# A state-space mixer and a two-layer attention stack: more scan buffers, the output projection and the layer norm's averages as products of rounded parts, new step orders

## The chip, the core and the metric

The kernel runs as one program on one core of a Trainium2 chip. TensorE (PE) multiplies matrices into eight PSUM banks; VectorE (DVE), ScalarE (ACT) and GpSimd (POOL) do the elementwise work; SyncE (SP) starts the transfers. Each engine works through its own list of instructions in the order in which it was written, and waits where a semaphore has not yet been raised. The metric is the time of one execution on the device in microseconds (us).

## What is computed

Sixteen sequences of 512 tokens with 256 features go through a modulated layer norm, a selective scan (the mixer), a second norm, and two layers of a block with windowed attention and a gated hidden layer. Cut to what the change touches:

```python
# the mixer: 512 inner channels, 16 states per channel
h = exp(dt * A) * h + (dt * B_t) * x_t          # for each channel and state, along 512 tokens
y_t = sum over the states of h * C_t
x = x + ga * (((y + x_ssm * D) * silu(z)) @ W_out.T)

# each of two layers
q, k, v = split(shift_token(x) @ wqkv)          # 8 heads of 64
q, k = rotary(l2norm(q) * qs), rotary(l2norm(k) * ks)
o = local_attention(q, k, v)                    # windows of 128 tokens
x = x + o @ wo                                  # 512 -> 256
h = shift_token(x)
h = (h - h.mean(-1)) / sqrt(h.var(-1) + 1e-5) * lg + lb
a, g = split(h @ w1 + b1)
x = x + (a * gelu(g)) @ w2 + b2
```

## The kernel before

There are two phases, one after the other. Features lie on the partitions, tokens along the free dimension, unless said otherwise.

**The scan phase** (`mixer_pass`) takes 16 sequences in a pipeline. A pass has steps of three neighbouring sequences. The work of a sequence is cut into 32 units of 2 states and 128 channels, so a unit is 128x1024 elements. For each unit ACT makes the decays (L684), the input term is made on DVE (`mul`, L737, from a row spread by PE, L565) for 22 units and on POOL (L806, from rows in `b_wide`) for 10, DVE scans (L755), POOL multiplies by C (`cmul`, L813, from rows in `c_wide`), and PE sums the states in PSUM (`sum`, L573). When half the units of a sequence are summed, DVE multiplies the sums by the gate (`gate`, L761), twice two of them in a sequence; the output product `out` (L492) needs all four. `DECAY_SLOTS`, `STATE_SLOTS`, `C_SLOTS` and `B_SLOTS` say how many buffers each kind has. The order of all steps is one table of names, `MIXER_ORDER` (L139): each engine takes from it those steps that are its own, in the table's order; a `-` behind a name means the sequence before.

**The layer phase** (`stack_pass`) runs 32 passes, 16 for each layer. A pass has again steps of three sequences: q, k and v and their rotation for the next one, attention for the present one, and the output projection and the hidden layer for the last one. The table `ORDER` (L830) sets the order, and `BANK_OF` (L844) which PSUM bank each product uses. The steps that matter here, with their engine:

- `pq`, `pk`, `v` (PE, L1296): six products of 128x512. A float32 factor is split beforehand in an upper part, rounded to the format `float32r`, and a lower part, the rest; upper times upper, upper times lower and lower times upper are summed. `ga` (L1407) and `wd` (L1428) do the same for the hidden layer.
- `psq` (ACT, L1459) squares q and k into `qk_sq`, which is the same buffer as `qk_rot`; `pss` (DVE, L1669) sums; `pnorm` (DVE, L1680) writes `qk`; `prot` multiplies by the rotary tables on POOL (L1601) and on DVE (L1695); `padd` (DVE, L1701) adds; `ptr` (PE, L1326) turns.
- `score` (PE, L1346), `mask` (DVE, L1728), `exp` (ACT, L1506), `rate` (DVE), `pn` (POOL, L1628), `pt` (PE, L1357, copied by ACT and DVE), `att` (PE, L1373), `onorm` (DVE, L1759: one copy into `o_t` for each of four windows).
- `wo` (PE, L1286): the output projection, for each of two halves of the features four products in full float32. `add` (DVE, L1766, L1770): the residual, and after the second half the sum of both halves.
- `mean` (PE, L1387) and `var` (PE, L1392): one product each in full float32, with a matrix whose elements are all 1/256. Between them `cen` (DVE, L1785), `sq` (ACT, L1527), `sqs` (DVE, L1774); after `var` come `dev` (ACT), `xn` (DVE), `hn` (ACT), `hns` (DVE, L1650 and L1652) and `ga`.

## Time and profile before

| | |
|---|---|
| median of 3 runs | 4311.34 us (4310.83 to 4312.2) |
| the profiled execution | 4316.54 us, of which the span of its instructions is 4314.5 us |
| busy over the span | PE 4052.9 us (94%), DVE 3679.9 (85%), ACT 2672.4 (62%), POOL 2639.3 (61%) |
| mean granted TensorE clock | 0.981 |

A page says of each engine how long it was busy; the stretches by window show that the two phases have different limits, so shares over the whole span mislead. The scan phase ends at about 1780 us, the layer phase has the rest. A row of a timeline gives start, length, engine, line, operation, and how many instructions are merged; in brackets the idle time ahead of it and what ended it. Lengths of matmuls overlap (each is listed until its result is written), so what a group of them costs is the distance from its start to the start of what follows.

### The profile page before, as it was taken

The page shows a single profiled execution, that of the slowest core. Times are in us where ns is not written, and L with a number is a line of the kernel's source. Part 1 is how long each engine was busy: PE and PEld are TensorE (multiplying, and loading weights), DVE is VectorE, ACT ScalarE, POOL GpSimd, SP SyncE. Part 2 cuts the span into 40 slices and gives each one's busy share as a digit, 9 for nine tenths or more (in the row PEclk, how much of TensorE's full clock was granted, in tenths as well). Part 3 has the DMA queues.
Part 4 walks back from the last instruction along what each step waited for, and adds up shares of the span by engine and source line. Part 5 has one row for each costly group of instructions (what it writes and reads, how often), then busy time and mean ns, then how long its engine had stood idle before and what let it go on. Part 6 is the DMA issues. An engine that isn't in the chain of part 4 may idle for free.

```text
span 4314.5 us, 60081 instructions
## 1 busy us (share of the span) xinstructions
PE 4052.9 (94%) x19614; PEld 2629.3 (61%) x19614; DVE 3679.9 (85%) x5981; ACT 2672.4 (62%) x5767; POOL 2639.3 (61%) x1297
## 2 busy tenths in 40 slices
...
GB/s 96 108 118 121 123 120 118 118 118 119 122 118 118 121 121 112 144 78 35 16 27 19 26 21 25 21 17 63 29 68 21 35 26 27 33 25 35 20 30 25
DMA packets 118499, 295.02 MB, mean 68 GB/s; under 512 B 21208, under 2 KB 43664, under 8 KB 118192
## 3 DMA queue, kind: packets, MB, share of 16 engines
...
q8 instruction: 160, 2.62, 0.3%
...
## 4 chain that ended last, share of the span: by engine, by line
PE 34%; DVE 14%; issue 4%; ACT 4%; DMA 1%; SPq 0%; POOL 0%; DVEq 0%; ACTq 0%
PE b_bank L1407 12%; PE b_bank L1428 6%; PE b_bank L1296 5%; PE b_bank L1357 3%; PE b_bank L1373 3%; PE b_bank L1286 3%; ACT b_scores L1506 2%; DVE b_scores L1728 2%; DVE b_qk L1680 2%; DVE b_qk_rate L1669 2%; PE b_bank L1326 1%; PE b_bank L1346 1%; DVE b_qk_rot L1695 1%; DVE b_qk_rot L1701 1%; DVE b_xc L1785 1%
## 5 line engine op out<-in xcount | busy, mean ns | idle before, releaser
L813 POOL TENSOR_TENSOR a_state<-a_state,a_c_wide 128x1024 f32<-128x1024 f32 x512 | 1196.0, 2369 | 37.4 <-DVE a_state L755 37.4
L1628 POOL TENSOR_TENSOR b_scores<-b_scores,b_row_rate 128x1024 f32<-128x1024 f32 (+1 forms) x256 | 426.5, 1682 | 969.6 <-DVE b_row_rate L1745 969.6
L573 PE MATMUL a_y_sum<-a_state,a_ident 128*128 128x512 f32 x2048 | 942.3, 598 | 0.7 <-POOL a_state L813 0.6
L755 DVE TENSOR_TENSOR_SCAN a_state<-a_decay,a_slot 128x1024 f32<-128x1024 f32 x352 | 788.9, 2271 | 1.9 <-ACT a_decay L684 0.6
L1296 PE MATMUL b_bank<-b_w_qkv,b_hx_part 128*128 128x512 f32 x2304 | 661.7, 426 | 35.2 <-DVE b_w_qkv L1830 16.2
L1506 ACT ACTIVATE b_scores<-b_scores,b_row_bias 128x256 f32<-128x256 f32 (+1 forms) x1024 | 478.0, 469 | 269.9 <-DVE b_row_bias L1734 269.9
L573 PEld LDWEIGHTS a_y_sum<-a_state,a_ident 128*128 128x128 f32 x2048 | 387.1, 191 | 401.0 <-issue 342.4
L684 ACT ACTIVATE a_decay<-a_dt,a_neg_a 128x512 f32<-128x512 f32 x704 | 458.8, 711 | 164.0 <-DVE a_state L755 163.8
L1407 PE MATMUL b_bank<-b_hn_part,b_w 128*128 128x512 f32 x2112 | 515.4, 399 | 25.6 <-DVE b_hn_part L1652 25.6
L1296 PEld LDWEIGHTS b_bank<-b_w_qkv,b_hx_part 128*128 128x128 f32 x2304 | 424.0, 193 | 157.7 <-issue 48.2
L1601 POOL TENSOR_TENSOR b_by_cos<-b_qk,b_rotary 128x1024 f32<-128x1024 f32 x128 | 336.7, 2631 | 252.0 <-DVE b_qk L1680 249.9
L1407 PEld LDWEIGHTS b_bank<-b_hn_part,b_w 128*128 128x128 f32 x2112 | 397.4, 189 | 134.4 <-DVE b_hn_part L1652 40.8
L737 DVE TENSOR_TENSOR a_slot<-a_u,a_slot 128x1024 f32<-128x1024 f32 x352 | 417.2, 1213 | 24.6 <-PE a_slot L565 24.5
L806 POOL TENSOR_TENSOR a_state<-a_u,a_b_wide 128x1024 f32<-128x1024 f32 x160 | 375.9, 2369 | 27.6 <-PE a_y_sum L573 26.4
L684 ACT ACTIVATE a_slot<-a_dt,a_neg_a 128x512 f32<-128x512 f32 x320 | 208.0, 682 | 273.1 <-DVE a_state L755 272.4
L1635 POOL TENSOR_TENSOR b_h_part<-b_h,b_h_part 128x512 fp32r<-128x512 f32 x160 | 205.2, 1291 | 267.9 <-ACT b_h_part L1571 267.9
L755 DVE TENSOR_TENSOR_SCAN a_state<-a_slot,a_state 128x1024 f32<-128x1024 f32 x160 | 357.9, 2269 | 6.7 <-ACT a_slot L684 6.4
L1728 DVE CUSTOM_DVE_ANT_0 b_scores<-b_bank,b_squares 128x256 f32<-128x256 f32 (+1 forms) x1024 | 337.5, 385 | 3.4 <-issue 3.4
L1428 PE MATMUL b_bank<-b_h_part,b_w 128*128 128x512 f32 x1088 | 296.2, 406 | 0.0
L1802 DVE SCALAR_TENSOR_TENSOR b_h<-b_bank,b_b_1a,b_gelu 128x512 f32<-128x512 f32 x192 | 143.4, 747 | 167.5 <-POOL b_h_part L1635 64.3
L565 PE MATMUL a_slot<-a_bc_parts,a_picks 96*128 96x512 bf16 x704 | 213.4, 386 | 69.0 <-DVE a_state L755 67.6
L1357 PE MATMUL b_bank<-b_squares,b_scores 128*128 128x128 f32 x1792 | 265.2, 277 | 12.3 <-DVE b_qk L1680 7.9
...
## 6 DMA issues: line engine op xcount, KB each, us to landing
a_c_wide<-bc_rows SPq DMA_DIRECT2D x256, 512.0 KB, 3.7
...
```

The source lines that it names most:

```text
L573: last = nc.tensor.matmul(y_sum[dd][:], ident[:], state[state_ring.slot[q]][:, i, :], start=False, stop=(j == GROUPS - 1 and i == GROUP - 1))
L684: last = nc.scalar.activation(to[:, i, :], dt[slot][:, d, :], ACT.Exp, scale=neg_a[:, d, n:n + 1])
L737: nc.vector.tensor_tensor(slots[q % 2][:], u[slot][:, d, :].unsqueeze(1).to_broadcast([P, GROUP, SEQ]), slots[q % 2][:], ALU.mult).then_in ...
L755: nc.vector.tensor_tensor_scan(flat(h), flat(factor), flat(term), 0.0, ALU.mult, ALU.add).then_inc(scan_done.sem, 1)
L813: nc.gpsimd.tensor_tensor(h[:], h[:], c_wide[c_ring.slot[q // 2]][:], ALU.mult).then_inc(cmul_done.sem, 1)
L1296: last = nc.tensor.matmul(psum.tile(name)[:], x[:, c, w * P:(w + 1) * P].bitcast(F32R), weights[:, c, cols:cols + INNER].bitcast(F32R), st ...
L1357: last = nc.tensor.transpose(psum.tile(name)[:, n * P:(n + 1) * P], scores[w % 2][:, h, blk * WINDOW:(blk + 1) * WINDOW], ident)
L1407: last = nc.tensor.matmul(psum.tile(f"{stem}{m}")[:], weights[:, c, at * P:(at + 1) * P].bitcast(F32R), x[:, c, :].bitcast(F32R), start=(n ...
L1428: last = nc.tensor.matmul(psum.tile(f"wd{m}")[:], weights[:, k, m * P:(m + 1) * P].bitcast(F32R), x[:, held, :].bitcast(F32R), start=(k == ...
L1506: e = nc.scalar.activation(scores[w % 2][:, h, lo:hi], scores[w % 2][:, h, lo:hi], ACT.Exp, bias=row_bias[:, w, h:h + 1], accum_out=row_su ...
L1628: nc.gpsimd.tensor_tensor(probs, probs, row_rate[:, w, at].unsqueeze(2).to_broadcast([P, 4, hi - lo]), ALU.mult)\
L1728: last = nc.vector.tensor_tensor_reduce(out=scores[w % 2][:, head, lo:hi], in0=psum.tile(f"s{w}_{g}_{h}")[:, at + lo:at + hi], in1=mask[:, ...
```

## The change

In the scan phase there are 4 decay buffers for 3, and 3 of each kind of row buffer for 2, and `MIXER_ORDER` is another table. In the layer phase `wo`, `mean` and `var` become sums of products in `float32r`: `wo` has 12 products a half for 4, `mean` and `var` 2 for 1 (the matrix has no lower part, since 1/256 is exact). So `onorm` becomes two instructions, a rounding copy by ACT and a subtraction by DVE; `add` and `sqs` get a rounding copy and a subtraction each on DVE; `w_o` is split once per layer. `qk_sq` is now the same buffer as `qk` rather than `qk_rot`. To make room, buffers share memory: the input rows `hx` with the upper part of the normalised rows, `x_res` with the lower part, and loads of `hx` and `x_res` wait for the last `ga` product that reads those. `ORDER` and `BANK_OF` are new.

```diff
-DECAY_SLOTS, STATE_SLOTS, C_SLOTS, B_SLOTS = 3, 6, 2, 2
+DECAY_SLOTS, STATE_SLOTS, C_SLOTS, B_SLOTS = 4, 6, 3, 3
...
-sum-:5 bcast-:10 sum-:6 mul-:12 mul-:13 xload:0 bcast-:11 scan-:12 cload-:13 cload-:14 cload-:15 scan-:13 cload:0
+scan-:10 scan-:11 cmul-:6 cmul-:7 scan-:12 scan-:13 bcast-:13 bcmid-:0 xT-:1 xs-:0 xscopy-:3 xs-:1 decay-:19 soft-:0
...
-qk_sq = qk_rot
+qk_sq = qk
...
+sum_parts, sq_parts = ([x[:, c, :] for c in range(CHUNKS)] for x in (hn_upper, hn_lower))
...
 def load_hx(s, slot, layer, _):
-    sp.wait_ge(v_done.sem, v_done.at(s))
+    if s < 3 or s == BATCH:
+        sp.wait_ge(v_done.sem, v_done.at(s))
+    if s >= 3:
+        sp.wait_ge(g_full.sem, g_full.at(s - 3, HID_CHUNKS))
...
 def load_res(s, slot, layer, _):
-    sp.wait_ge(x2_done.sem, x2_done.at(s))
     if s == BATCH:
+        sp.wait_ge(x2_done.sem, x2_done.at(s))
         load_w_o(1)
+    if s > 0:
+        sp.wait_ge(g_full.sem, g_full.at(s - 1, HID_CHUNKS))
...
 def project_out(s, slot, layer, m):
-    product(s, f"wo{m}", w_o, m * P, [o_t[:, p, :] for p in range(PAIRS)])
+    parts = [(weights, x, p) for weights, x in ((w_o[0], upper), (w_o[1], upper), (w_o[0], lower)) for p in range(PAIRS)]
+    for n, (weights, x, p) in enumerate(parts):
+        last = nc.tensor.matmul(psum.tile(f"wo{m}")[:].rearrange("p (a f) -> p a f", a=2),
+                                weights[:, p, m * P:(m + 1) * P].bitcast(F32R), x[p].bitcast(F32R),
+                                start=(n == 0), stop=(n == len(parts) - 1))
...
+def averaged(s, name, parts):
+    for n, x in enumerate(parts):
+        last = nc.tensor.matmul(psum.tile(name)[:], mean_mat[:].bitcast(F32R), x.bitcast(F32R), start=(n == 0), stop=(n == 1))
...
 def square_qk(s, slot, layer, w):
-            act.wait_ge(qk_sum_done.sem, qk_sum_done.at(s, w))
+            act.wait_ge(by_cos_done.sem, by_cos_done.at(s, w))
+            act.wait_ge(by_sin_done.sem, by_sin_done.at(s, 2 * w))
...
+def copy_out(s, slot, layer, w):                      # on ACT
+    nc.scalar.activation(o_upper[:, :, w * WINDOW:(w + 1) * WINDOW].bitcast(F32R),
+                         psum.tile(f"o{w}")[:].rearrange("p (n c) -> p n c", c=WINDOW), ACT.Copy).then_inc(o_upper_done.sem, 1)
...
 def copy_out(s, slot, layer, w):                      # on DVE
-    nc.vector.tensor_copy(o_t[:, :, w * WINDOW:(w + 1) * WINDOW], psum.tile(f"o{w}")[:].rearrange("p (n c) -> p n c", c=WINDOW))\
-        .then_inc(o_t_done.sem, 1)
+    dve.wait_ge(o_upper_done.sem, o_upper_done.at(s, w + 1))
+    nc.vector.tensor_tensor(o_lower[:, w // 2, :, at:at + WINDOW].bitcast(F32R),
+                            psum.tile(f"o{w}")[:].rearrange("p (n c) -> p n c", c=WINDOW),
+                            o_upper[:, :, w * WINDOW:(w + 1) * WINDOW], ALU.subtract).then_inc(o_t_done.sem, 1)
...
 def cut_hx_of(s):
+    if s > 0:
+        dve.wait_ge(v_full.sem, v_full.at(s - 1, TILES))
...
 def times_sin(s, slot, layer, w):
+    dve.wait_ge(k_t_full.sem, k_t_full.at(s, w))
...
+def cut_sum(s, x, parts, signal):                     # called by add_residual and add_squares
+    upper, lower = parts
+    dve.wait_ge(signal.sem, signal.at(s, 1))
+    nc.vector.tensor_copy(upper.bitcast(F32R), x).then_inc(signal.sem, 1)
+    dve.wait_ge(signal.sem, signal.at(s, 2))
+    nc.vector.tensor_tensor(lower.bitcast(F32R), x, upper, ALU.subtract).then_inc(signal.sem, 1)
```

**First place, DVE in the scan phase, where one sequence's last units end.** `a_slot<-a_u,a_slot` is `mul`, `a_state<-...` a scan, `a_u<-a_y_sum,a_sz` a `gate`. Before:

```order
L737 TENSOR_TENSOR a_slot<-a_u,a_slot 128x1024 x2
L755 SCALAR_TENSOR_TENSOR a_state<-a_decay,a_slot 128x1024 x2
L737 TENSOR_TENSOR a_slot<-a_u,a_slot 128x1024 x2
L761 TENSOR_TENSOR a_u<-a_y_sum,a_sz 128x512
L755 SCALAR_TENSOR_TENSOR a_state<-a_decay,a_slot 128x1024
L761 TENSOR_TENSOR a_u<-a_y_sum,a_sz 128x512
```

and now:

```order
L738 TENSOR_TENSOR a_slot<-a_u,a_slot 128x1024 x2
L756 SCALAR_TENSOR_TENSOR a_state<-a_decay,a_slot 128x1024 x2
L738 TENSOR_TENSOR a_slot<-a_u,a_slot 128x1024
L756 SCALAR_TENSOR_TENSOR a_state<-a_decay,a_slot 128x1024
L738 TENSOR_TENSOR a_slot<-a_u,a_slot 128x1024
L762 TENSOR_TENSOR a_u<-a_y_sum,a_sz 128x512 x2
```

The next sequence's first scan has moved from between the two gates to ahead of both. In PE's list the last three sums stood behind both of the next sequence's first spreads; now they stand between and behind them.

**Second place, DVE in the layer phase, from `cen` to `sqs`.** Before:

```order
L1785 TENSOR_TENSOR b_xc<-b_x,b_bank 128x512 x2
L1708 COPY b_k_t<-b_bank 128x4x128
L1725 MEMSET b_waiter 128x1
L1728 ISA b_scores,b_row_max<-b_bank,b_squares 128x256
L1728 ISA b_row_max 128x1
...
L1774 TENSOR_TENSOR b_h<-b_h 128x512
L1669 TENSOR_REDUCE b_qk_rate<-b_qk_rot 128x16
```

and now:

```order
L1865 TENSOR_TENSOR b_xc<-b_x,b_bank 128x512 x2
L1788 MEMSET b_waiter 128x1
L1791 ISA b_scores,b_row_max<-b_bank,b_squares 128x256
L1791 ISA b_row_max 128x1
...
L1804 COPY b_probs_t<-b_bank 128x512 x2
L1756 TENSOR_TENSOR b_qk_rot<-b_qk,b_rotary 128x16x32 x2
L1853 TENSOR_TENSOR b_h<-b_h 128x512
L1847 CAST b_hn_part_16562<-b_h 128x512
L1849 TENSOR_TENSOR b_hn_part_16562<-b_h,b_hn_part_16562 128x512
```

Between `cen` and the squares' sum there stood one copy and one mask step; now a mask step, two copies and the rotation's sine products, and the cut of the sum follows it.

**Third place, PE in the layer phase, from `mean` to `var`.** Before:

```order
L1387 MATMUL b_bank<-b_rstd,b_squares 128x512
L1296 MATMUL b_bank<-b_w_qkv,b_hx_part 128x512 x6
L1326 MATMUL b_bank<-b_squares,b_qk_rot 128x128 x8
L1296 MATMUL b_bank<-b_w_qkv,b_hx_part 128x512 x6
L1357 MATMUL b_bank<-b_squares,b_scores 128x128 x4
L1296 MATMUL b_bank<-b_w_qkv,b_hx_part 128x512 x6
L1357 MATMUL b_bank<-b_squares,b_scores 128x128 x4
L1392 MATMUL b_bank<-b_h,b_squares 128x512
```

and now:

```order
L1429 MATMUL b_bank<-b_hn_part_16561,b_mean_mat 128x512 x2
L1381 MATMUL b_bank<-b_k_t,b_q_t 128x256 x4
L1392 MATMUL b_bank<-b_squares,b_scores 128x128 x16
L1329 MATMUL b_bank<-b_w_qkv,b_hx_part 128x512 x18
L1429 MATMUL b_bank<-b_hn_part_16562,b_mean_mat 128x512 x2
L1408 MATMUL b_bank<-b_probs_t,b_v 64x128 x8
```

All 16 turns of a window's probabilities now stand ahead of `var`, with 18 products of q, k and v, and the turn of q and k has moved behind it.

## Rows read from the trace of the kernel before

**Rows 1.** By window of 200 us: busy us of each engine, clock, DMA:
```profile
1000.00:1200.00 200.00, 188.13 (x566) 92.34 (x566) 194.73 (x126) 141.69 (x244) 193.08 (x88) 1.00 0.37 119
2400.00:2600.00 200.00, 197.52 (x1191) 148.74 (x1190) 166.60 (x411) 126.84 (x331) 81.00 (x46) 1.00 0.06 19
```

**Rows 2.** Waits from 300 to 1500 us: engine, for whom, us in total, times:
```profile
DVE a_u L761 <- PE a_y_sum L573: 20.0, 11, 1.9
DVE a_slot L737 <- PE a_slot L565: 6.6, 13, 1.4
POOL a_state L806 <- PE a_y_sum L573: 21.0, 19, 1.5
POOL a_state L813 <- DVE a_state L755: 18.5, 34, 0.8
```

**Rows 3.** Timeline of DVE, scan phase, a gate in two neighbouring passes; then POOL:
```profile
605.56 0.69 DVE L761 TENSOR_TENSOR a_u<-a_y_sum,a_sz 128x512 f32<-128x512 f32 x1 [1.89 <-PE a_y_sum L573]
711.81 0.69 DVE L761 TENSOR_TENSOR a_u<-a_y_sum,a_sz 128x512 f32<-128x512 f32 x1 [1.88 <-PE a_y_sum L573]
705.58 4.68 POOL L813 TENSOR_TENSOR a_state<-a_state,a_c_wide 128x1024 f32<-128x1024 f32 x2 [0.74 <-DVE a_state L755]
```

**Rows 4.** Waits of PE and DVE from 2000 to 4200 us:
```profile
PE b_bank L1407 <- DVE b_hn_part L1652: 16.2, 29, 0.6
DVE b_qk_rate L1669 <- ACT b_qk_rot L1459: 107.9, 59, 2.4
```

**Rows 5.** Timeline of PE, layer phase, one pass:
```profile
2210.91 11.45 PE L1407 MATMUL b_bank<-b_hn_part,b_w 128*128 128x512 f32 x48 [0.57 <-DVE b_hn_part L1652]
2249.81 3.70 PE L1286 MATMUL b_bank<-b_o_t,b_w_o 128*128 128x512 f32 x8
2252.94 3.36 PE L1296 MATMUL b_bank<-b_w_qkv,b_hx_part 128*128 128x512 f32 x12
2256.24 2.00 PE L1346 MATMUL b_bank<-b_k_t,b_q_t 64*128 64x256 f32 x16
2264.26 1.10 PE L1387 MATMUL b_bank<-b_rstd,b_squares 128*128 128x512 f32 x2
2266.64 1.44 PE L1326 MATMUL b_bank<-b_squares,b_qk_rot 128*128 128x128 f32 x8
2269.75 1.64 PE L1296 MATMUL b_bank<-b_w_qkv,b_hx_part 128*128 128x512 f32 x6
2271.22 0.60 PE L1357 MATMUL b_bank<-b_squares,b_scores 128*128 128x128 f32 x4
2271.66 1.02 PE L1392 MATMUL b_bank<-b_h,b_squares 128*128 128x512 f32 x2
2272.61 1.13 PE L1346 MATMUL b_bank<-b_k_t,b_q_t 64*128 64x256 f32 x8
2285.23 4.94 PE L1407 MATMUL b_bank<-b_hn_part,b_w 128*128 128x512 f32 x20 [0.55 <-DVE b_hn_part L1652]
```

**Rows 6.** Timeline of DVE in the same pass:
```profile
2250.52 0.69 DVE L1650 CAST b_hx_part<-b_hx 128x1024 fp32r<-128x1024 f32 x1
2264.03 1.29 DVE L1695 TENSOR_TENSOR b_qk_rot<-b_qk,b_rotary 128x512 f32<-128x512 f32 x2
2267.03 0.64 DVE L1741 COPY b_probs_t<-b_bank 128x512 f32<-128x512 f32 x1
2267.59 1.27 DVE L1785 TENSOR_TENSOR b_xc<-b_x,b_bank 128x512 f32<-128x512 f32 x2
2269.39 0.42 DVE L1728 CUSTOM_DVE_ANT_0 b_scores<-b_bank,b_squares 128x256 f32<-128x256 f32 x1
2270.78 0.71 DVE L1774 TENSOR_TENSOR b_h<-b_h 128x512 f32<-128x512 f32 x1
```

**Rows 7.** Timelines of DVE and of POOL, a sine product beside a cosine product:
```profile
2293.75 3.96 DVE L1695 TENSOR_TENSOR b_qk_rot<-b_qk,b_rotary 128x512 f32<-128x512 f32 x2
2294.30 2.85 POOL L1601 TENSOR_TENSOR b_by_cos<-b_qk,b_rotary 128x1024 f32<-128x1024 f32 x1
```

More of the change, by code:

```diff
@@ new lines @@
+mul-:27 cmul-:27 scan-:26 scan-:27 decay:8 sum-:24 bcast-:29 mul-:28 sum-:25 mul-:29 sum-:26 bcast-:30 mod:1 up:1
+sum-:27 scan-:28 bcast-:31 cload:7 scan-:29 dt-:1 mul-:30 sum-:28 cload:8 bcast:0 dtadd-:0 sum-:29 bcast:1 mul-:31
+sum-:30 decay:9 cmul-:28 scan-:30 cload:9 scan-:31 cmul-:29 sum-:31 bload:12 decay:10 decay:11 cmul-:30 dev2:0 mul:0
+skip:0 scan:0 mul:1 xcopy:1 out:0 bcast:2 gate-:2 gate-:3 xscopy:0 scan:1 decay:12 bcast:3 cload:10 scan:2 h2store:0
+cmul-:31 scan:3 sum:0 mul:2 res:0 bcast:4 bcast:5 out:1 mul:3 decay:13 cmul:0 sum:1 mul:4 cmul:1 h2:0 mean2:0 mul:5
@@ L160 @@
+bcast:6 xscopy:1 decay:14 dtadd-:1 cmul:2 cmul:3 scan:4 decay:15 xT:0 cstore:0 bcast:7 bcast:8 res:1 scan:5 cen2:0
+cload:11 sum:2 cmul:4 hT:0 mul:6 sum:3 cload:12 hT:1 mul:7 scan:6 hcut:0 cmul:5 sum:4 scan:7 xscopy:2 bccopy:0
+bload+:1 sum:5 bload+:4 decay:16 bcast:9 var2:0 bcast:10 cload:13 scan:8 sum:6 mul:8 scan:9 mul:9 mul:10 xn2:0 mul:11
+hcut:1 decay:17 bcast:11 cload:14 sum:7 bcup:0 decay:18 bcast:12
 """
@@ L829 @@
 ORDER = """
-ptr-:3 mask:0.0 mask:0.1 att-:3 score:0.0 exp:0 pn:0.0 hxs:0 hxload:0 psq:0 score:0.1 score:1.0 wo:0 mask:1.0 add:0
-prate:0 rate:0 pss:0 pnorm:0 pq:0 pk:0 pn:0.1 resload:0 score:1.1 mask:1.1 add:1 prot:0 score:2.0 exp:1 padd:0 wo:1
-pn:1.0 rate:1 v:0 pt:0.0 pt:0.1 cen:0 vc:0 ptc:0 sq:0 psq:1 mean:0 pk:1 ptr:0 pn:1.1 mask:2.0 sqs:0 pq:1 pt:1.0 v:1
-prate:1 pss:1 pt:1.1 vc:1 dev:0 pnorm:1 var:0 mask:2.1 score:2.1 pt:1.2 v:2 pt:1.3 pk:2 prot:1 xn:0 att:0 onorm:0
-att:1 padd:1 mask:3.0 score:3.0 vc:2 hn:0 exp:2 hns:0 gelu:0 score:3.1 onorm:1 psq:2 mask:3.1 ptr:1 gated:0 rate:2
@@ L835 @@
[L835 to L839 removed]
+ptr-:3 v-:3 hxs:0 mask:1.0 vc-:3 mask:1.1 score:0.0 score:0.1 score:1.0 hxload:0 exp:0 rate:0 add:0 pss:0 score:1.1
@@ new lines @@
+wo:0 psq:0 pk:0 x1load:0 pq:0 add:1 exp:1 rate:1 wo:1 v:0 pnorm:0 prate:0 v:1 pt:0.0 pn:0.0 pn:0.1 pt:0.1 vc:0 mean:0
+score:2.0 pt:1.0 cen:0 pn:1.0 mask:2.0 resload:0 pt:1.1 pn:1.1 store:0 sq:0 pt:1.2 pt:1.3 prot:0 psq:1 vc:1 pq:1 sqs:0
+pss:1 padd:0 xn:0 mask:2.1 pk:1 dev:0 v:2 prate:1 vc:2 var:0 ptc:0 hns:0 hn:0 pnorm:1 att:0 mask:3.0 score:2.1 onorm:0
+onorm:1 prot:1 rate:2 padd:1 gated:0 ptr:0 pn:2.0 gated:1 hl:0 pss:2 outstore:0 exp:2 mask:3.1 gelu:0 gelu:1 psq:2
+pn:2.1 pq:2 hl:1 gated:2 pnorm:2 att:1 score:3.0 hh:0 hh:1 gelu:2 pn:3.0 prate:2 hl:2 ptc:1 exp:3 prot:2 rate:3 ga:0
```

193 lines of the change are left out of this document (114 added, 79 removed).

## The prediction

> **What bounds the kernel now.** I read the windows first, because the two phases differ. In the scan phase three engines are nearly full at once: of 200 us DVE is busy for 194.7, POOL for 193.1 and PE for 188.1. In the layer phase only PE is: 197.5, beside 166.6 for DVE, 126.8 for ACT and 81.0 for POOL [rows 1]. So a microsecond of PE is worth nothing by itself in the first phase and nearly a microsecond in the second, where TensorE is also at its full clock, 1.00 [rows 1].
>
> The waits say what is left in the scan phase. A pass takes 711.81 - 605.56 = 106.25 us [rows 3]. In 1200 us, 11.3 passes, DVE waits 20.0 us for PE ahead of a gate and 6.6 us ahead of a `mul`, that is 1.8 and 0.6 us a pass; POOL waits 39.5 us, 3.5 a pass [rows 2]. DVE is the nearest to its bound: without waits its pass is 106.25 - 2.4 = 103.8 us, POOL's 102.8.
>
> A pass of the layer phase is 2285.23 - 2210.91 = 74.32 us from the first `ga` to the next one's first [rows 5]. PE waits about 0.57 us of it, at one place: ahead of `ga`, for DVE's cut of the normalised rows (16.2 us in 29 passes) [rows 4, 5]. So its work is 73.75 us. DVE waits a good deal, for instance 107.9 us for squares [rows 4], and no one is late through it.
>
> **What the PE work becomes.** The price of a `float32r` product is read from 48 of them in 11.45 us, 0.239 us each [rows 5]. The first half of `wo` and 12 such products take 2256.24 - 2249.81 = 6.43 us; less 12 x 0.239 = 2.87, four float32 products cost 3.56 us [rows 5]. Twelve `float32r` products will cost 2.87. That saves 0.69 us a half, 1.4 a pass. `mean` and six products take 2.38 us, so `mean` alone costs 2.38 - 1.43 = 0.95, and `var` 2272.61 - 2271.66 = 0.95 [rows 5]. Two products will cost 0.48: 0.47 us saved twice, 0.9 a pass. The sum is 2.3 us. Where products of this kind stand in small groups they cost a little more: six in 2271.22 - 2269.75 = 1.47 us, 0.245 each [rows 5]; by that price the saving is 2.1. I take 2.2 us a pass (ends 2.0 and 2.4), so PE's work becomes 71.55 us. Should PE wait as little as now, 32 passes give 70 us.
>
> **What DVE and ACT get.** The cut of a sum is a rounding copy of 512 elements and a subtraction. The copy of 1024 elements took 0.69 us [rows 6]; half of it lies between 0.35 and 0.69, I take 0.42, since the time of start is a small part there. The subtraction is like the sum of squares, 0.71 [rows 6]. Two cuts a pass are 2.2 us. `onorm` on DVE stays one instruction of 512 elements from PSUM. DVE's share rises from 83% of 74.3 us, 61.9 us, to 64.1 of some 73 us, 88%: no bound yet, but less slack. ACT gets four copies; a copy of that shape on DVE takes 0.64 [rows 6] and I take the same, 2.6 us a pass, which its 37% idle time takes [rows 1]. The split of `w_o` is a copy and a subtraction once per layer, 2 us each, at most 4 us in all; I take 1.
>
> **Where PE could wait now.** The saving is paid out only if the products find their factors ready. Between `mean` and `var` DVE has a chain. After `mean` (0.48 us) come `cen` 1.27, a mask step 2270.78 - 2269.39 = 1.39, two copies of 0.56 (2267.59 - 2267.03), sine products 1.29, the sum of squares 0.71 and its cut 0.42 + 0.71: 7.4 us [rows 6]. The squares on ACT are hidden beside the mask and the copies. PE has in the same stretch `mean` 0.48, eight score products 1.1, sixteen turns at 0.44 for four, 1.8, and eighteen products at 0.24, 4.4: 7.8 us [rows 5]. So the two are nearly even, where DVE had in the old order only `cen`, a copy and a mask step between, and PE 2271.66 - 2264.26 = 7.40 us [rows 5]. There is no slack to speak of, and every wait of DVE in this stretch will be PE's. Behind it, from `var` to `ga`, the same steps are as before, with less PE work between (the old stretch was 12.6 us [rows 5]). For `var`, `ga` and the turns of the probabilities, which now come sooner behind their exponentials, I take 1.3 us of waiting a pass in place of 0.57. The lower end is 0.6, as now; the upper is 3.2, if one of DVE's steps is blocked once a pass by POOL as in rows 7 (below).
>
> The layer pass then is 71.55 + 1.3 = 72.85 us, 1.47 less than now, and 32 passes give 47 us. The ends are 74.32 - (71.35 + 0.6) = 2.4 us a pass, 76 in all, and 74.32 - (71.75 + 3.2) = -0.6, a loss of 20.
>
> The other new waits are covered. The squares of q and k now wait for both rotary products of the window before, a chain of some 7 us a window, while four windows share 73 us. The cut of the input rows waits for the last `v` product, which PE has done before the scores, and DVE has two mask steps on those scores ahead of it. Loads of `hx` and `x_res` wait for the last `ga`, some 30 us ahead of their use.
>
> **What the scan phase becomes.** The engines' work is the same; only waits can go. At the gate, DVE in the old order had two `mul` steps after the last scan and then waited 1.88 us for PE, whose sums stood behind two spreads [rows 3]. In the new order a scan of another sequence stands ahead of both gates, and PE's sums come one spread sooner. The wait of 1.88 us goes. What is late next is the output product, since both gates are done some 1 us later; it has three scans of cover. The `mul` waits (0.6 us a pass) and POOL's waits for DVE [rows 2] I leave as they are, though more buffers for decays and rows let ACT and SP run further ahead; neither was the last to arrive in any row here. I take 1.5 us a pass, 24 us over 16 passes. The ends are 2.4 us, all of DVE's waits, 38 in all, and a loss of 10 us if the new order opens as large a wait at another place.
>
> **The sum.** 4316.5 us of the profiled execution, less 47, less 24, plus 1, is 4246.5. The median of the runs shown lies 5.2 us below that execution, so I forecast 4241 us.
>
> **Rivals.**
> *Layer phase without gain.* The chain from `mean` to `var` and the turns take back what the products save, in waits of 2.8 us a pass in place of 0.57. For it: the even balance above. Against it: rows 4 show that a chain of the same kind, just as tight, costs PE 0.57 us. The time is 4311 - 24 = 4287 us.
> *Both gains whole.* 4311 - 76 - 38 = 4197 us. Against it: the waits would have to shrink in both phases.
> *The scan order loses.* Some 5 us lost there and 47 won: 4269 us.
> *Slower, by blocking between DVE and POOL.* Two sine products that take 1.29 us took 3.96 where POOL's cosine product ran [rows 6, 7]: 2.67 us lost. The new cuts are DVE steps of that kind, both operands in SBUF, and the sine products now stand just ahead of the squares' sum, at the time of POOL's cosine product of the same window. If one such block a pass falls on the chain, the pass is 71.55 + 0.57 + 2.67 = 74.8 us, 15 us more over 32 passes, and with the scan's 24 the time is 4302, no change. If there are two, one at each chain, it is 77.5 us, 100 us more: 4387. It decides from 2.8 us of waiting a pass for the phase, and 3.5 for the whole. Against it: the sine products of rows 6 took their 1.29 us, so a block is not the rule, and POOL is busy for only 81 of 200 us here [rows 1].
> The Trainium skill, page "SBUF — State Buffer", section "SBUF: two separate sides", says that the port pair which VectorE and GpSimd share is an exclusive lock, taken by a VectorE step in a two-port mode or with two SBUF inputs for its whole length. Rows 7 agree with it. By that rule the rounding copies, and not only the subtractions, can be blocked; the sum stays, and the rule speaks for this last rival.
> *The saving is not there:* the products in `float32r` cost more with the new operands than rows 5 show. Then only the scan's gain is left, less the waits: near 4300.
>
> **How the numbers follow.** The forecast case has 0.60, 4241 us with 4205 to 4280; the layer phase without gain 0.12; both gains whole 0.06; the scan order losing 0.06; one block a pass, or no saving, 0.07; two blocks or another loss of that size 0.09. A measurement of this kernel can tell about 0.2%, 8.6 us. So faster has 0.60 + 0.12 + 0.06 + 0.06 = 0.84, the same 0.07, slower 0.09. The range of 4200 to 4293 holds the forecast case, the first and third rival, and some of the second: 0.8.
>
> **What would show it.** The scan pass should be near 104.7 us with no wait of 1.88 at the gates; the layer pass near 72.9. `wo` should cost 2.9 us a half, `mean` and `var` 0.5. PE's waits ahead of `var`, `ga` and the turns should sum to 1.3 us a pass; over 2.8 is the first rival, and sine products or cuts that last over 2 us are the fourth. The forecast is wrong if the scan pass is not under 105.5 us or the layer pass not under 73.8.

## The result, and the profile after

| | before | changed kernel |
|---|---|---|
| median | 4311.77 us (4310.83 to 4315.74, 4 runs) | 4197.57 us (4192.46 to 4202.05, 4 runs) |
| ratio, 95% interval | 1 | 0.9733 [0.9716, 0.975] |
| span of the profiled execution | 4314.5 us | 4192.1 us |

The kernel is 2.7% faster, 114 us by the medians. The forecast was 4241 us, and the range of 4200 to 4293 misses the time by 2.4 us. The rival "both gains whole" stood at 4197 with a chance of 0.06: its number is what came out, though not from the terms that it was added up from, as the part on the miss shows.

The two profiled executions are 122.4 us apart. The layer phase opens with a memset of VectorE, which starts at 1798.56 us before and at 1752.98 us now:

```profile
1752.98 0.06 DVE L1897 MEMSET b_hx<- 128x1 f32 x1 [4.72 <-PEq L225]
```

So 45.6 us come from the scan phase and its start, and 76.8 us from the layer phase. About 5 of the 45.6 lie ahead of the first gate, which DVE reaches at 130.52 us before and at 125.30 now; the last section shows that as much can lie between two executions with the same instructions up to there. The same windows as in [rows 1], busy us of PE, PEld, DVE, ACT, POOL:

```profile
1000.00:1200.00 200.00, 192.87 (x573) 93.48 (x572) 199.35 (x128) 139.91 (x244) 198.64 (x90) 1.00 0.37 122
2400.00:2600.00 200.00, 199.13 (x1251) 157.93 (x1248) 165.16 (x445) 136.80 (x348) 88.17 (x49) 1.00 0.06 19
```

In the scan phase DVE is idle for 0.65 us in 200 where it had 5.3. In the layer phase PE is idle for 0.9 where it had 2.5. The clock is 1.00 in both, so it is no part of the difference.

**Scan phase.** DVE's timeline, the two gates that answer to [rows 3], in neighbouring passes:

```profile
588.66 1.28 DVE L762 TENSOR_TENSOR a_u<-a_y_sum,a_sz 128x512 f32<-128x512 f32 x2
692.33 1.27 DVE L762 TENSOR_TENSOR a_u<-a_y_sum,a_sz 128x512 f32<-128x512 f32 x2
```

Both gates run back to back, with no idle time in brackets: the wait of 1.88 us is gone. The pass is 692.33 - 588.66 = 103.67 us for 106.25. The waits from 300 to 1500 us, that answer to [rows 2] (all that is left of DVE's, and two of POOL's):

```profile
DVE a_slot L738 <- PE a_slot L566: 2.8, 12, 0.2
POOL a_state L814 <- DVE a_state L756: 6.1, 11, 0.6
POOL a_state L807 <- PE a_y_sum L574: 2.8, 12, 0.3
```

**Layer phase.** PE's timeline of one pass, and the start of the next, that answers to [rows 5] (`wo` is L1422, `mean` and `var` L1429, `ga` L1457):

```profile
2329.70 2.13 PE L1422 MATMUL b_bank<-b_o_upper,b_w_o 128*128 128x512 f32 x8
2331.66 1.09 PE L1422 MATMUL b_bank<-b_o_lower,b_w_o 128*128 128x512 f32 x4
2332.59 2.96 PE L1329 MATMUL b_bank<-b_w_qkv,b_hx_part 128*128 128x512 f32 x12
2335.39 2.03 PE L1422 MATMUL b_bank<-b_o_upper,b_w_o 128*128 128x512 f32 x8
...
2342.27 0.72 PE L1429 MATMUL b_bank<-b_hn_part,b_mean_mat 128*128 128x512 f32 x2 [0.25 <-ACT b_probs_t L1569]
...
2350.39 0.70 PE L1429 MATMUL b_bank<-b_hn_part,b_mean_mat 128*128 128x512 f32 x2
2351.02 1.09 PE L1408 MATMUL b_bank<-b_probs_t,b_v 128*64 128x128 f32 x16
...
2358.50 5.85 PE L1457 MATMUL b_bank<-b_hn_part,b_w 128*128 128x512 f32 x24
...
2414.18 0.72 PE L1429 MATMUL b_bank<-b_hn_part,b_mean_mat 128*128 128x512 f32 x2 [0.25 <-ACT b_probs_t L1569]
```

The pass is 2414.18 - 2342.27 = 71.91 us; it was 74.32. A half of `wo` costs 2332.59 - 2329.70 = 2.89 us. `mean` costs 0.65 and `var` 0.63 by the distance to the next start. There is no idle time ahead of `var` and none ahead of `ga`; the one wait that is left stands ahead of `mean`, 0.25 us, for a copy of turned probabilities by ACT, which uses the same PSUM bank. PE's waits from 2000 to 4100 us say the same of 28 passes; the second line holds two passes in which PE did wait for the cut:

```profile
PE b_bank L1429 <- ACT b_probs_t L1569: 7.0, 28, 0.3
...
PE b_bank L1429 <- DVE b_hn_part L1849: 4.6, 2, 2.7
```

One pass is unlike the others. Where the first layer ends and the second begins, the new kernel takes 78.4 us from `cen` to `cen` (2846.51 to 2924.91) in place of 71.9, while the old one has 74.3 there (2862.36 to 2936.69) as elsewhere. PE stands idle for 4.71 us in it:

```profile
2912.86 4.58 PE L1329 MATMUL b_bank<-b_w_qkv,b_hx_part 128*128 128x512 f32 x12 [4.71 <-issue]
```

The profile names no releaser. Every kernel here with the new layer order has such a wait of 3.9 to 6.0 us, and the old order has none; what causes it wasn't tested.

DVE between `mean` and `var`, that answers to [rows 6]:

```profile
2343.03 1.29 DVE L1865 TENSOR_TENSOR b_xc<-b_x,b_bank 128x512 f32<-128x512 f32 x2
...
2346.82 1.62 DVE L1756 TENSOR_TENSOR b_qk_rot<-b_qk,b_rotary 128x512 f32<-128x512 f32 x2
2348.38 0.68 DVE L1853 TENSOR_TENSOR b_h<-b_h 128x512 f32<-128x512 f32 x1
2349.09 0.43 DVE L1847 CAST b_hn_part<-b_h 128x512 fp32r<-128x512 f32 x1
2349.55 0.69 DVE L1849 TENSOR_TENSOR b_hn_part<-b_h,b_hn_part 128x512 fp32r<-128x512 f32 x1
```

The cut of the squares' sum ends at 2350.24, and `var` starts at 2350.39. The chain is as tight as the prediction had it, yet PE doesn't wait for it. Whether that is luck or slack is what the third group of experiments asks.

### The profile page after: what moved, and what is told of

It reads as the page before. It is cut to its first block, busy times and chain, and to the rows that moved or that the text cites. A ratio compares the mean times of both kernels' runs of the same rounds, so it can differ in the third digit from the quotient of the medians.

```text
span 4192.1 us, 61075 instructions
## 1 busy us (share of the span) xinstructions
PE 3987.2 (95%) x19870; PEld 2671.8 (64%) x19870; DVE 3628.0 (87%) x6114; ACT 2745.0 (65%) x5896; POOL 2671.1 (64%) x1298
## 4 chain that ended last, share of the span: by engine, by line
PE 52%; DVE 2%; ACT 1%; DMA 1%; issue 1%; POOL 1%; SPq 0%; DVEq 0%; ACTq 0%; POOLq 0%
PE b_bank L1329 12%; PE b_bank L1457 12%; PE b_bank L1478 6%; PE b_bank L1408 5%; PE b_bank L1381 5%; PE b_bank L1392 4%; PE b_bank L1422 4%; PE b_bank L1361 3%; PE b_bank L1429 1%; DMA b_hx<-stack_rows 1%; ACT b_probs_t L1569 0%; PE b_bank L1493 0%; DVE b_qk_rot L1756 0%; DVE b_hx_part L1711 0%; POOL b_scores L1687 0%
## 5 line engine op out<-in xcount | busy, mean ns | idle before, releaser
L1687 POOL TENSOR_TENSOR b_scores<-b_scores,b_row_rate 128x1024 f32<-128x1024 f32 (+1 forms) x256 | 458.1, 1801 | 816.3 <-DVE b_row_rate L1808 816.3
L756 DVE TENSOR_TENSOR_SCAN a_state<-a_decay,a_slot 128x1024 f32<-128x1024 f32 x352 | 788.6, 2270 | 0.7
L1329 PE MATMUL b_bank<-b_w_qkv,b_hx_part 128*128 128x512 f32 x2304 | 602.0, 406 | 32.1 <-DVE b_w_qkv L1910 17.7
L1660 POOL TENSOR_TENSOR b_by_cos<-b_qk,b_rotary 128x1024 f32<-128x1024 f32 x128 | 310.9, 2429 | 478.7 <-DVE b_qk L1740 474.7
L1457 PE MATMUL b_bank<-b_hn_part,b_w 128*128 128x512 f32 x2112 | 531.4, 402 | 6.3 <-DVE b_hn_part L1711 6.2
L1457 PEld LDWEIGHTS b_bank<-b_hn_part,b_w 128*128 128x128 f32 x2112 | 387.2, 189 | 114.4 <-issue 20.2
L1510 ACT ACTIVATE b_qk<-b_bank 128x512 f32<-128x512 f32 x256 | 142.5, 597 | 251.0 <-PE b_bank L1329 176.8
L1694 POOL TENSOR_TENSOR b_h_part<-b_h,b_h_part 128x512 fp32r<-128x512 f32 x160 | 237.4, 1484 | 79.8 <-ACT b_h_part L1630 79.7
```

The lines of the kernel that those rows point to most:

```text
L756: nc.vector.tensor_tensor_scan(flat(h), flat(factor), flat(term), 0.0, ALU.mult, ALU.add).then_inc(scan_done.sem, 1)
L1329: last = nc.tensor.matmul(psum.tile(name)[:], x[:, CHUNKS - 1 - c, w * P:(w + 1) * P].bitcast(F32R), weights[:, c, cols:cols + INNER].bitc ...
L1457: last = nc.tensor.matmul(psum.tile(f"{stem}{m}")[:], weights[:, c, at * P:(at + 1) * P].bitcast(F32R), x[:, c, :].bitcast(F32R), start=(n ...
L1687: nc.gpsimd.tensor_tensor(probs, probs, row_rate[:, w, at].unsqueeze(2).to_broadcast([P, 4, hi - lo]), ALU.mult)\
```

## Experiments

All are timed against the kernel before on the same chip. Between the groups of runs the median of that kernel goes from 4311.8 to 4316.8 us, so a distance between the medians of two groups can be off by some 5 us; the length of a pass is steadier. A time difference divided by 32 is about that of one layer pass, by 16 that of one scan pass.

### Which half brings what

*scan_only*: the kernel before with the new `MIXER_ORDER` and buffers.

```diff
-DECAY_SLOTS, STATE_SLOTS, C_SLOTS, B_SLOTS = 3, 6, 2, 2
+DECAY_SLOTS, STATE_SLOTS, C_SLOTS, B_SLOTS = 4, 6, 3, 3
...
-sum-:5 bcast-:10 sum-:6 mul-:12 mul-:13 xload:0 bcast-:11 scan-:12 cload-:13 cload-:14 cload-:15 scan-:13 cload:0
+scan-:10 scan-:11 cmul-:6 cmul-:7 scan-:12 scan-:13 bcast-:13 bcmid-:0 xT-:1 xs-:0 xscopy-:3 xs-:1 decay-:19 soft-:0
```

> The kernel before with the scan phase of the changed one (its table and its 4, 3 and 3 buffers), the layer phase as it was. In the trace of the changed kernel the layer phase's first step of DVE stands at 1753.1 us, in the one before at 1798.6 (45.5 us earlier), and the scan pass is 103.67 us in place of 106.25. Theory (the two gains are independent and add up): 45 us less than before, near 4266. Rival (the scan phase's gain is paid by both, for instance because the layer phase's start or its memory layout gave part of it): under 35 us.

Measured: 4272.43 us, ratio 0.9903 [0.9888, 0.9918], against 4313.58 us of before: 41 us won.

*layer_only*: the changed kernel with the old `MIXER_ORDER` and buffers.

```diff
-DECAY_SLOTS, STATE_SLOTS, C_SLOTS, B_SLOTS = 4, 6, 3, 3
+DECAY_SLOTS, STATE_SLOTS, C_SLOTS, B_SLOTS = 3, 6, 2, 2
...
-scan-:10 scan-:11 cmul-:6 cmul-:7 scan-:12 scan-:13 bcast-:13 bcmid-:0 xT-:1 xs-:0 xscopy-:3 xs-:1 decay-:19 soft-:0
+sum-:5 bcast-:10 sum-:6 mul-:12 mul-:13 xload:0 bcast-:11 scan-:12 cload-:13 cload-:14 cload-:15 scan-:13 cload:0
```

> The changed kernel with the scan phase of the one before (its table and 3, 2 and 2 buffers). Theory (independent gains): 77 us less than before, near 4235, with a layer pass of 71.9 us. Rival: a part of the gain belongs to the scan phase, then under 65 us.

Measured: 4236.55 us, ratio 0.9822 [0.9807, 0.9836]: 77 us won. Its gates still wait as in [rows 3]:

```profile
499.63 0.69 DVE L762 TENSOR_TENSOR a_u<-a_y_sum,a_sz 128x512 f32<-128x512 f32 x1 [1.88 <-PE a_y_sum L574]
```

The halves add up, 41 + 77 = 118 us, beside 114 for both together, and the executions of the changed kernel alone lie 10 us apart. So no help or hindrance between the phases can be seen. Each gain is a little above the upper end that the prediction gave it: 41 for 38, 77 for 76.

### The scan phase: order or buffers?

*slots_only*: the kernel before, with more buffers alone.

```diff
-DECAY_SLOTS, STATE_SLOTS, C_SLOTS, B_SLOTS = 3, 6, 2, 2
+DECAY_SLOTS, STATE_SLOTS, C_SLOTS, B_SLOTS = 4, 6, 3, 3
```

> The kernel before with 4 decay buffers and 3 of each kind of row buffer, in its old order. Theory (no wait in the old order was for a buffer of these kinds, it is the order alone that brings the gain): within 4 us of the kernel before, the gate's wait of 1.88 us stays. Rival (the buffers let ACT and SP run ahead, and that takes the waits away): 20 us or more less.

Measured: 4314.18 us over 10 runs, ratio 1.0003 [0.9994, 1.0012], nothing. DVE's wait at the gates from 300 to 1500 us is that of [rows 2] again:

```profile
DVE a_u L761 <- PE a_y_sum L573: 20.0, 11, 1.9
```

*three_decays*: the changed kernel, with the fourth decay buffer alone taken away.

```diff
-DECAY_SLOTS, STATE_SLOTS, C_SLOTS, B_SLOTS = 4, 6, 3, 3
+DECAY_SLOTS, STATE_SLOTS, C_SLOTS, B_SLOTS = 3, 6, 3, 3
```

> The changed kernel with 3 decay buffers in place of 4; row buffers stay at 3 (with 2 of them the new order can't run to its end). Theory (the fourth decay buffer is of no use, ACT being ahead anyway): within 4 us of the changed kernel, a scan pass of 103.7 us. Rival (the new order runs long rows of scans for which the decays must be ready): scans wait for decays, 10 to 40 us more than the changed kernel.

Measured: 4233.2 us, ratio 0.9815 [0.9799, 0.9831]: 36 us of the scan phase's 41 are gone again. The theory, that the fourth buffer is of no use, is refuted, and the rival holds. DVE's timeline, gate and next scan, and its waits from 300 to 1500 us:

```profile
602.87 1.28 DVE L762 TENSOR_TENSOR a_u<-a_y_sum,a_sz 128x512 f32<-128x512 f32 x2
608.67 4.47 DVE L756 TENSOR_TENSOR_SCAN a_state<-a_slot,a_state 128x1024 f32<-128x1024 f32 x2 [2.33 <-ACT a_slot L685]
...
DVE a_state L756 <- ACT a_slot L685: 25.7, 11, 2.3
```

The gates don't wait, so the order does its part, but 2.33 us a pass come back a few steps later: a scan waits for its decays, which ACT writes late. Since the buffer count is all that was changed, it is the missing buffer that makes them late. So neither edit does much by itself, 0 us for the buffers and some 5 for the order: the order puts a scan of another sequence ahead of the gates, and that scan's decays need somewhere to lie. What the third row buffer of each kind is worth wasn't measured; by the author's account the new order cannot run to its end with two, which no run here shows.

### The layer phase: products or order?

Three kernels put back products of full float32 in the changed kernel and leave all steps of DVE and ACT in place.

*wo_full*: `wo` as four float32 products a half. The kernel leaves out the lower parts of both factors.

```diff
-parts = [(weights, x, p) for weights, x in ((w_o[0], upper), (w_o[1], upper), (w_o[0], lower)) for p in range(PAIRS)]
+parts = [(w_o[0], upper, p) for p in range(PAIRS)]
...
-                                            weights[:, p, m * P:(m + 1) * P].bitcast(F32R), x[p].bitcast(F32R),
+                                            weights[:, p, m * P:(m + 1) * P], x[p],
```

> The changed kernel with the output projection as four products a half in full float32 again; the cuts, the copies and the order stay. It leaves out the lower part of the attention's result (its factor is the rounded one), so the output is a little off. In the traces a half of wo took 2.89 us in the changed kernel and 3.47 to 3.56 in the one before. Theory (the price of the products is the gain, PE having no other wait): 2 x 0.6 to 0.7 us a pass, 37 to 43 us more than the changed kernel. Rival (PE's saved time would only have been waiting for DVE): under 20 us more.

*mean_full*: `mean` and `var` as one float32 product each.

```diff
-averaged(s, "mean", sum_parts)
+psum.filled(nc.tensor.matmul(psum.tile("mean")[:], mean_mat[:], x2_sum[:], start=True, stop=True), "mean")
...
-averaged(s, "var", sq_parts)
+psum.filled(nc.tensor.matmul(psum.tile("var")[:], mean_mat[:], sq[:, 0, :], start=True, stop=True), "var")
```

> The changed kernel with mean and var as one product each in full float32, of the uncut sums; the cuts stay on DVE and PE waits for them as before. In the traces mean cost 0.65 and var 0.63 us in the changed kernel, 0.95 and 0.95 in the one before. Theory: 0.3 us each, 19 us more than the changed kernel. Rival by the prediction's term (a pair costs 0.48): 0.47 each, 30 us more. Rival (the wait ahead of var hides it): 0 to 10 us more.

*both_full*: both edits.

> Both edits of the two runs before this one: the new order and its cuts with all products in full float32; it leaves out the lower part of the attention's result. Its distance from the kernel with only the layer phase changed back is what the new layer order is worth by itself. Theory (products bring 57 to 62 us of the 77): 4254 to 4260, and 15 to 20 us come from the order (PE's wait of 0.57 us ahead of the hidden layer gone: 18 us). Rival (the products bring all 77): 4275.

| | median us | ratio | median above 4197.57 | span above 4192.1 | a pass |
|---|---|---|---|---|---|
| changed kernel | 4197.57 | 0.9733 | | | 71.90 |
| wo_full | 4234.77 | 0.981 [0.9795, 0.9825] | 37.2 | 40.9 | 73.17 |
| mean_full | 4214.3 | 0.9768 [0.9753, 0.9782] | 16.7 | 20.8 | 72.43 |
| both_full | 4249.33 | 0.9843 [0.9827, 0.986] | 51.8 | 57.5 | 73.69 |

The spans are those of single executions. The profiled one of the changed kernel is among its fastest, so they overstate the distances by a few us. A pass is half the distance between a `mean` of PE and the second `mean` behind it, between 2270 and 2435 us.

PE's timelines of `wo_full`, a half of `wo` and twelve products to the next half, and of `mean_full` (L1437 is its `mean`, L1442 its `var`):

```profile
2342.74 3.70 PE L1422 MATMUL b_bank<-b_o_upper,b_w_o 128*128 128x512 f32 x8
2345.87 3.34 PE L1329 MATMUL b_bank<-b_w_qkv,b_hx_part 128*128 128x512 f32 x12
2349.05 3.59 PE L1422 MATMUL b_bank<-b_o_upper,b_w_o 128*128 128x512 f32 x8
```

```profile
2355.34 1.02 PE L1442 MATMUL b_bank<-b_h,b_mean_mat 128*128 128x512 f32 x2
2356.29 1.09 PE L1408 MATMUL b_bank<-b_probs_t,b_v 128*64 128x128 f32 x16
```

A half of `wo` and what follows take 2349.05 - 2342.74 = 6.31 us here and 2335.39 - 2329.70 = 5.69 in the changed kernel: 0.62 a half, 64 halves, 40 us. The pass says the same, 73.17 - 71.90 = 1.27 us, and so do the times, 37 and 41. `var` costs 0.95 in full float32 and 0.63 as two products, 0.32 us; 64 such groups would give 20 us. The pass grows by 0.53 only, which is 17 us, as by the medians.

Both together are 1.79 us a pass, 57 us; the medians give 52. 4249.33 us lies below the 4254 to 4260 of the theory, and the rival's 4275 is further off. So the order is worth a little more than was expected: its share is 19 us by the spans (76.8 - 57.5), 22 by the passes (74.37 - 73.69 = 0.68 each), and 23 by the medians of `scan_only` and `both_full`. This share also holds the bank table, the buffer change of `qk_sq` and the added cuts and copies, which `both_full` keeps. Two passes of each kernel show where it lies: the kernel before from 2041.20 to 2189.94 us, and `both_full`, from `mean` to `mean`; the first number is the stretch, the second PE's busy time.

```profile
2041.20:2189.94 148.74, 147.08 (x913) 111.54 (x913) 122.78 (x303) 90.86 (x234) 60.07 (x34) 1.00 0.06 22
2285.42:2432.80 147.38, 146.88 (x913) 111.63 (x913) 118.30 (x311) 95.60 (x241) 62.19 (x35) 1.00 0.07 23
```

The same 913 products keep PE busy for 147.1 and 146.9 us, but it is idle for 1.66 us of two passes before and 0.50 in `both_full`. So 0.58 us of the order's 0.68 a pass is idle time that went. The exchange the other way round, the new products in the old layer order, wasn't tried.

### Is the chain from `mean` to `var` really even?

If it is, work of DVE added to it must cost PE its own length, from the first instruction on. *chain_one* makes the rounding copy of the squares' sum twice.

```diff
+                dve.wait_ge(sq_added.sem, sq_added.at(s, 1))
+                for i in range(1):
+                    nc.vector.tensor_copy(sq_parts[0].bitcast(F32R), sq[:, 0, :]).then_inc(sq_added.sem, 1)
+                    dve.wait_ge(sq_added.sem, sq_added.at(s, 2 + i))
```

> The changed kernel with the rounding copy of the squares' sum made twice, one after the other: 0.46 us more on DVE between mean and var. In the trace of the changed kernel the cut's last instruction ends at about 2350.2 us and var starts at 2350.39, straight behind the products ahead of it. Theory (the prediction's balance holds: no slack, each added wait is PE's): 0.3 to 0.45 us a pass, 10 to 14 us more than the changed kernel. Rival (there is slack that the sum of rows missed): within 3 us.

*chain_three*: three more copies, `range(3)`.

> As the run before, with three more copies, 1.4 us more on DVE between mean and var. Theory (no slack): 1.2 to 1.4 us a pass, 38 to 45 us more than the changed kernel. Rival (slack of about 1 us): 10 to 15 us more.

*copy_elsewhere*: a copy of the same size once a pass, ahead of the fourth gated product, where DVE has time.

```diff
+                if m == 3 and s > 0:
+                    nc.vector.tensor_copy(rstd[:], rstd[:])
```

> The changed kernel with one more copy of 512 elements on DVE, in place on a buffer that is free then, ahead of the fourth gated product of a pass, where DVE waits 2.8 us a pass for ACT. Both theories of the last two runs: within 3 us of the changed kernel, since it falls into a wait. If DVE's load as such were what counts, it would cost 10 to 14 us as in the chain.

| | median us | ratio | median above 4197.57 | span above 4192.1 | a pass |
|---|---|---|---|---|---|
| copy_elsewhere | 4195.28 | 0.9721 [0.9707, 0.9734] | -2.3 | -0.8 | 71.90 |
| chain_one | 4212.59 | 0.9757 [0.9744, 0.9771] | 15.0 | 19.1 | 72.41 |
| chain_three | 4242.4 | 0.983 [0.9816, 0.9843] | 44.8 | 52.6 | 73.37 |

PE's waits for the cut from 2000 to 4100 us, first in `chain_one`, then in `chain_three`:

```profile
PE b_bank L1429 <- DVE b_hn_part L1849: 15.9, 28, 0.6
```

```profile
PE b_bank L1429 <- DVE b_hn_part L1849: 41.8, 28, 1.5
```

A copy costs nothing elsewhere. On the chain the first costs 0.51 us a pass (72.41 - 71.90), and two more cost 0.48 each. By PE's waits it is 0.57 and then (41.8 - 15.9) / 28 / 2 = 0.46 each. A rounding copy holds up the step behind it by 0.46 us (2349.09 to 2349.55 in the changed kernel). So the first copy is paid in full, and the chain has no slack that this can find. By the medians `chain_three` is within its 38 to 45 us and `chain_one` 1 us above its 10 to 14.

### Is the last wait of PE a loss?

*mean_bank0*: `mean` in a bank that ACT's copy doesn't use.

```diff
-v0:5 mean:3 pt0_1:6 v1:2
+v0:5 mean:0 pt0_1:6 v1:2
```

> The changed kernel with the mean's product in bank 0 in place of bank 3, which it shares with ACT's copies of the turned probabilities. Its trace shows PE waiting 0.25 us a pass ahead of the mean's product for the copy of turned probabilities, 28 waits summing 7.0 us between 2000 and 4100. If that wait is a true loss of the path, 32 passes give 0.25 * 32 = 8 us back: near 4189 us, 0.2% below the changed kernel. If it only moves to another place of the pass, or VectorE's even chain takes it over, the time stays within 2 us of 4197.

Measured: 4199.9 us, ratio 0.9726 [0.9713, 0.9739], no difference from the changed kernel. PE's timeline and waits:

```profile
2347.88 0.71 PE L1429 MATMUL b_bank<-b_hn_part,b_mean_mat 128*128 128x512 f32 x2
...
2351.19 1.06 PE L1392 MATMUL b_bank<-b_squares,b_scores 128*128 128x128 f32 x8 [0.40 <-POOL b_scores L1687]
...
PE b_bank L1392 <- POOL b_scores L1687: 11.3, 28, 0.5
```

The wait ahead of `mean` is gone; behind it PE waits 0.40 us for POOL's scaled scores, which in the changed kernel arrive in the time that ACT's copy takes up. A pass is 2347.88 - 2275.99 = 71.89 us, as in the changed kernel. The median is 2.3 us above the changed kernel's, a little more than the 2 us allowed, but the pass has not changed, so the second theory holds. The 0.25 us are no gain by themselves: PE would have to find three things ready earlier, ACT's copy, POOL's scores and DVE's cut.

## Why the prediction missed its range

**Where the gains come from: right.** The wait at the gates went, the products pay on PE almost in full, and the chain from `mean` to `var` is as even as counted: forecast 7.4 us for DVE and 7.8 for PE, measured 2350.24 - 2342.27 = 7.97 and 2350.39 - 2342.27 = 8.12, and `chain_one` shows that nothing is spare. PE's waits name none of the other added steps of DVE and ACT, apart from 2.3 us in all, in five waits, for the cut of `hx`. Cuts of 512 elements take 0.43 and 0.69 us, forecast 0.42 and 0.71.

**PE's work: the sum right, its parts not.** It went down by (147.08 - 143.23) / 2 = 1.9 us a pass, forecast 2.2:

```profile
2270.38:2414.18 143.80, 143.23 (x929) 114.35 (x929) 118.95 (x311) 95.42 (x241) 62.14 (x35) 1.00 0.07 23
```

`wo` saves 1.27 us by the pass of `wo_full` (forecast 1.4). `mean` and `var` save 0.62 by their distances and 0.53 by the pass of `mean_full` (forecast 0.9): a pair that stands alone costs 0.64 us, not twice 0.239. The price from a group of 48 [rows 5] holds for twelve products and not for two. The prediction saw that six cost more each and didn't follow that down to two. This error alone would have made the time longer than forecast.

**PE's waits: the step that failed.** "I take 1.3 us of waiting a pass in place of 0.57", with a lower end of 0.6, "as now". Measured: (143.80 - 143.23) / 2 = 0.28 us of idle time, 0.25 of it ahead of `mean`, none ahead of `var`, `ga` or the turns; before it was (148.74 - 147.08) / 2 = 0.83, of which a named wait showed 0.57. So where 0.73 us more were forecast, 0.55 went: 1.28 us a pass, 41 us in all. The products take 0.3 us a pass of that back, 9 us, and the rest, 32, is about the miss of the layer phase (77 measured, 47 forecast). The fit is partly chance: what the uneven passes lose, the slow one between the layers and the last two, is about what the stretch from the memset to the first `cen` gains, 158.8 us for 171.6.

The error is one of reading. "Every wait of DVE in this stretch will be PE's" is true, and was shown, but an even chain is one that costs nothing as it stands, and the waits of DVE in it had yet to be found. The old wait of 0.57 us ahead of `ga` was taken as a floor, with the words "from `var` to `ga`, the same steps as before". That is wrong of DVE's list. In the old one the normalisation `xn` (L1790) stands behind other work, and the cut of the normalised rows (L1652) behind a mask step. DVE's timeline before, from the same pass as [rows 6]:

```profile
2276.17 1.08 DVE L1734 TENSOR_SCALAR b_row_bias<-b_row_max 128x8 f32<-128x8 f32 x1
...
2278.97 1.21 DVE L1790 TENSOR_TENSOR b_xc<-b_xc,b_rstd 128x1024 f32<-128x1024 f32 x1
...
2283.95 1.22 DVE L1652 TENSOR_TENSOR b_hn_part<-b_xc,b_hn_part 128x1024 fp32r<-128x1024 f32 x1
```

and now (`xn` is L1870, the cut L1711):

```profile
2352.62 1.22 DVE L1870 TENSOR_TENSOR b_xc<-b_xc,b_rstd 128x1024 f32<-128x1024 f32 x1
...
2356.68 1.23 DVE L1711 TENSOR_TENSOR b_hn_part<-b_xc,b_hn_part 128x1024 fp32r<-128x1024 f32 x1
```

From the start of `var` to the end of that cut there were 2285.17 - 2271.66 = 13.5 us, and now there are 2357.91 - 2350.39 = 7.5. PE's own work between went down too, from 13.0 us to 8.1, but DVE is now done 0.6 us ahead of `ga`.

**The scan phase: the second step that failed.** 1.5 us a pass was taken of 2.4 that seemed to be there. Measured are 106.25 - 103.67 = 2.58. The `mul` waits (0.6 us) fell to 0.2 as well (2.8 us in 11.6 passes). And the end of 2.4 was no end: the busy row has DVE idle for 5.3 us in 200, 2.8 a pass [rows 1], while the waits named in [rows 2] sum to 2.4. The reason given for leaving the rest, that buffers for decays and rows were never last to arrive, was true of the old order alone: `three_decays` shows that the new one would have lost 36 of its 41 us without the fourth.

**The first rival** (waits of 2.8 us in the layer phase) and **the third** (the scan order loses) did not happen.

**Blocking between DVE and POOL** did not reach the cuts. Durations in ns (shortest, median, longest) of all sine products before and now, then of the cuts of the squares' sum:

```profile
L1695 DVE TENSOR_TENSOR b_qk_rot<-b_qk,b_rotary x256: 673/683/3941, 1817.1 to 4190.1; 128x512 f32<-128x512 f32 x128
```

```profile
L1756 DVE TENSOR_TENSOR b_qk_rot<-b_qk,b_rotary x256: 675/681/3349, 1772.3 to 4070.8; 128x512 f32<-128x512 f32 x128
...
L1849 DVE TENSOR_TENSOR b_hn_part<-b_h,b_hn_part x32: 691/692/694, 1918.2 to 4150.3; 128x512 fp32r<-128x512 f32 x32
```

No such subtraction is more than 2 ns from the median, nor is a rounding copy (426 to 428 ns). On the chain only a little of it is left: the two sine products above took 1.62 us for 1.29, while POOL's cosine product was at work from 2344.88 to 2347.30:

```profile
2344.88 2.42 POOL L1660 TENSOR_TENSOR b_by_cos<-b_qk,b_rotary 128x1024 f32<-128x1024 f32 x1
```

Taken over the kernel the change does the opposite of what the rival feared. The same sine products as groups, busy us and mean ns behind the bar, before and now:

```profile
L1695 DVE TENSOR_TENSOR b_qk_rot<-b_qk,b_rotary 128x512 f32<-128x512 f32 x256 | 260.4, 1057 | 1.2
```

```profile
L1756 DVE TENSOR_TENSOR b_qk_rot<-b_qk,b_rotary 128x512 f32<-128x512 f32 x256 | 188.8, 777 | 2.6 <-PE b_bank L1361 1.3 <-issue 1.3
```

Mean less median is 0.374 us before and 0.096 now, times 256: 96 us of DVE's time before, and 25 now. Of those that took over 60 ns more than the median, 67 before and 38 now, each overlaps a step of POOL; of the others only 7 and 3 do. So this is blocking. It hits other steps of DVE too. The small step on the row maxima took 611 ns in the mean before for a median of 173, and 245 now; the sum behind the rotation, hardly blocked before (1248 ns for 1217), now takes 1455 for 1225:

```profile
L1734 DVE TENSOR_SCALAR b_row_bias<-b_row_max 128x8 f32<-128x8 f32 x128 | 78.2, 611 | 4.4
```

```profile
L1762 DVE TENSOR_TENSOR b_qk_rot<-b_qk_rot,b_by_cos 128x1024 f32<-128x1024 f32 x128 | 186.2, 1455 | 2.9 <-POOL b_by_cos L1660 1.8
```

With the rates' small step (349 ns for 174 before, 313 for 175 now) the four groups lost 178 us before and lose 81 now. The rival was judged by one row, the products of [rows 6] that took their 1.29 us; the group's mean would have told that the old order was blocked often and that a new one had something to win. The 97 us that went, 3 a pass, are the larger part of why DVE is busy for 59.4 us a pass (83%, 165.16 of 200 us) and not the 64.1 that were worked out. One blocked step stood on the path to `ga`: the row-maxima step at 2276.17 above, ahead of `xn`, takes 1.08 to 1.12 us there in 30 of 31 passes before and 0.17 in all of them now. These 0.9 us are more than the wait of 0.57. So the gain ahead of `ga` may come in part from blocking that went; no run separates it from the shorter list. By the Trainium skill, page "SBUF — State Buffer", section "SBUF: two separate sides", such a lock lasts as long as the step that holds it. The trace agrees: the longest sine product now takes 3.35 us, starts at 1843.42 during a step of POOL, and ends 0.56 us behind it:

```profile
1842.71 3.50 POOL L1675 TENSOR_TENSOR b_w_whole<-b_w_whole,b_h_part 128x1536 fp32r<-128x1536 f32 x1
```

**The range.** Its lower end was put at 4200 to leave out a rival of 4197 whose two halves were taken to be unlikely together. The two halves are alike, in that both are waits that vanish when each is given its cover; that they had to go together is not shown. That the time came to 4197 is in part luck. The rival took PE's work at its lowest and a wait of 0.6 us, and the scan's waits at 2.4; measured are less saved work, a wait of 0.28, and 2.58.
